# Cross-attention on one core: the context products of two groups in one set of 512-column matmuls, and scaling factors spread from rows written four times

## The chip, the cores and the metric

The kernel runs on one core of a Trainium2 chip. The core's engines work at the same time, each through its own instructions in order: TensorE (PE, matmuls), VectorE (DVE), ScalarE (ACT), GpSimd (POOL) and SyncE (SP), which here issues every DMA. They wait for each other through semaphores. The metric is the device time of one launch in microseconds (us). Three runs of the kernel before gave 676.45 us as their median, from 675.78 to 676.48.

## The reference, cut to what matters

Eight batches of 256 queries and 256 keys of width 1024; 32 query heads of width 32 share 8 key/value heads, so four query heads form a group with one key/value head. LoRA terms are added to each weight.

```python
q = _lora_linear(hidden_states, Wq, Aq, Bq)     # (8, 256, 1024): 32 heads of 32
k = _lora_linear(traces, Wk, Ak, Bk)            # (8, 256, 256):   8 heads of 32
v = _lora_linear(traces, Wv, Av, Bv)
scores = jnp.einsum('bhqd,bhtd->bhqt', q, k) / jnp.sqrt(HD)
attn = jax.nn.softmax(scores, axis=-1)
context = jnp.einsum('bhqt,bhtd->bhqd', attn, v)
out = _lora_linear(context, Wo, Ao, Bo)
return hidden_states + out
```

## The kernel before, in words

**Units and slots.** A group of four heads in one batch is a unit `u`; there are 8 per batch, 64 in all. A unit takes four slots `c = 0..3`, a batch has 32 slots `s`, and each engine has its own function `slot(b, s, ...)` that says what it does in a slot, in this order:

- PE: `scores_t` (L1519: the transposed scores of unit `u-1`, one matmul of 512 columns); the slot's share of the projections (`group_step`, L1482 and L1484: three matmuls of 256 columns and three of 512); if `c == 0` the context product of unit `u-2` (`context`, L1524 to L1537); then `scores` for four slots ahead (L1502: two matmuls of 256 columns).
- ACT: `exp_turned` (L941: the exponentials of the transposed scores, into `probs_t`); in some slots `proj_high` (L914, L919: the high part of a projected group); `exps` for three slots ahead (L930: exponentials with row sums).
- DVE: `row_max` for three slots ahead (L1142); at `c == 0` `split_max` and `turn_max` (L1151, L1153, L1163), which also turn the reciprocals of the unit before; at `c == 3` `reciprocal` (L1170) and `normalize` of unit `u-2` (L1177); then `proj_lows` (for k L1126 and L1129, for q L1134 and L1136: the low part of a projected group, after ACT's high part); in slots 15, 16, 18 and 19 `input_low` (L1183).
- POOL: `place_max` at `c == 1`, the splitting of the inputs, and one copy of v per batch.

**Projection groups.** A batch projects twelve groups (`BODY`: q4 to q7 of the batch, then k0, k1, q0 to q3, v0, v1 of the next), each 24 steps deep, nine steps in a slot. They alternate between two PSUM banks. So the first matmul of group `j` waits on `proj_out` until DVE has written the low part of group `j-2` (L1616). Group 4 (k0) has its low part written in DVE's slot 17; group 6 (q0) starts in PE's slot 19. Group 7 (q1) has its low part written in slot 25; group 9 (q3) starts in slot 27. In batch 0 the same holds.

**The context product.** Two key tiles times four heads: eight fp32 matmuls `128x32` by `128x256`, which the trace shows as sixteen instructions. Each head has its own 32 columns of the array (`tile_position=(0, HD * h)`) and lands in its own 32 rows of one half of a PSUM bank (`ctx_bank`). `probs_t` holds two units. `normalize` multiplies the 128x256 result by `scales` into `ctx_stage`, and `store_ctx` writes it to DRAM.

**The scaling factors.** The reciprocals of the row sums are turned into four rows of 256. `put_rows` writes them to DRAM (L535), and `spread` reads them back with each row repeated for 32 partitions (L543): four outermost rows, 128 pieces of 1 KB.

**Stages.** Up to about 54 us the weights are prepared. The units' steady work runs to about 460 us, batch 0 to 6. Then comes batch 7, in which the output weights are prepared as well (its own order, `last_body`). From about 535 us the output products of batches 1 to 7 run (L1543, L1677).

Of the kernel before, what the change touches and what calls it, by code (L numbers as in the profile page):

```python
# [27 lines left out]
P = 128  # L28
NB = 8
S = 256  # L30
D = 1024
KT = D // P
HD = 32
NG = 8
GH = 4
# [59 lines left out]
SUM_RING = 4  # L95


def xattn(nc, xt, ct, xn, wq, wkv, wo, akv, bkv, aq, bq, a4o, b4o, out):
    with ExitStack() as ctx:
# [44 lines left out]
        def rows_of(tile, rows):  # L144
# [27 lines left out]
                          for i in range(2))  # L172
# [8 lines left out]
        ctx_bank = banks[:, 4, 0:S]  # L181
# [4 lines left out]
        r_dram = nc.dram_tensor("r_rows", [2, GH, S], F32, kind="Internal").ap()  # L186
# [76 lines left out]
        block = ctx.enter_context(nc.Block())  # L263

# [130 lines left out]
        def _(sp):  # L395
# [118 lines left out]
            def body(b, first, last):  # L514
# [4 lines left out]

                def store_ctx(g):  # L520
                    if first and g < 0:
                        return
                    wait(ctx_done, unit0 + (g + 1))
                    row = ctx_dram[b, g] if g >= 0 else ctx_dram[b - 1, g + NG]
                    sp.dma_start(row, ctx_stage[:, g % 2]).then_inc(ctx_stored[g % 2], DMA)
# [6 lines left out]
                def put_rows(g):  # L532

                    wait(turned_out, unit0 + (g + 2))
                    sp.dma_start(r_dram[g % 2], turned_sb[KM:KM + GH, (g + 1) % 2]).then_inc(r_stored[g % 2], DMA)  # L535

                def spread(g):

                    if first and g < 0:
                        return  # L540
                    wait(r_stored[g % 2], b * (4 * DMA) + DMA * (g // 2 + 1))
                    need(sp, ctx_done, unit0 + (g - 1))
                    sp.dma_start(scales[:, g % 2], r_dram[g % 2].unsqueeze(1).broadcast_to([GH, HD, S])  # L543
                                 ).then_inc(r_spread[g % 2], DMA)
# [13 lines left out]
                store_ctx(-2)  # L558
# [5 lines left out]
                spread(0)  # L564
                store_ctx(-1)
                stack_q(4, fills + 3, st0 + 4)
                put_rows(1)
                load_x(1)
                send(pos["q", 5, 0])
                load_x(2)  # L570
                spread(1)
                send(pos["q", 6, 0])
                store_ctx(0)
                stack_q(5, fills + 3, st0 + 8)
                put_rows(2)
                load_x(3)
                spread(2)
                send(pos["q", 7, 0])
                store_ctx(1)
                stack_q(6, fills + 4, st0 + 12)  # L580
                load_context(b + 2, 0)
                put_rows(3)
                load_context(b + 2, 1)
                load_context(b + 2, 2)
                send(pos["k", 0, 1])
                spread(3)
                load_context(b + 2, 3)
                store_ctx(2)
                send(pos["k", 1, 1])
# [3 lines left out]
                spread(4)  # L593
                send(pos["q", 0, 1])
                store_ctx(3)
                stack_q(0, fills + 5, st0 + 20)
                put_rows(5)
                send(pos["q", 1, 1])
                spread(5)
                store_ctx(4)  # L600
                send(pos["q", 2, 1])
                stack_q(1, fills + 5, st0 + 24)
                put_rows(6)
                spread(6)
                send(pos["q", 3, 1])
                store_ctx(5)
                stack_q(2, fills + 6, st0 + 28)
                put_rows(7)
                if b == NB - 2:
# [284 lines left out]
        def _(act):  # L894
# [40 lines left out]
            def exp_turned(b, u, j):  # L935

                t, hp = divmod(j, 2)
                act.wait_ge(st_mm, b * SLOTS + (4 * u + j + 1))
                if j == 0:
                    need(act, ctx_mm, b * NG + (u - 1))  # L940
                nc.scalar.activation(  # L941
                    probs_t[:, u % 2, t, 2 * hp:2 * hp + 2, :].rearrange("p a b -> p (a b)"),
# [124 lines left out]
        def _(dve):  # L1067
# [105 lines left out]
            def normalize(b, u):  # L1173
# [3 lines left out]
                nc.vector.tensor_tensor(ctx_stage[:, u % 2, :], ctx_bank, scales[:, u % 2, :],  # L1177
                                        ALU.mult).then_inc(ctx_done, 1)

# [112 lines left out]
            def slot(b, s, first, last):  # L1292
# [20 lines left out]
                if c == 3 and not (first and u < 2):  # L1313
                    normalize(b, u - 2)
# [113 lines left out]
        def _(pe):  # L1428
# [95 lines left out]
            def context(b, u):  # L1524
# [5 lines left out]
                for t in range(2):  # L1530
                    for h in range(GH):
                        last = nc.tensor.matmul(  # L1532
                            ctx_bank[HD * h:HD * (h + 1), :],
# [207 lines left out]
```

## Time and profile before

| | |
|---|---|
| median of 3 runs | 676.45 us |
| the profiled execution: its own time | 678.06 us |
| the profiled execution: span of its instructions | 676.3 us |
| mean granted TensorE clock | 0.947 |
| PE busy | 662.5 us, 98% of the span |
| DVE busy | 512.7 us, 76% |
| ACT busy | 467.6 us, 69% |
| POOL busy | 375.9 us, 56% |

The span runs from the first to the last instruction of the profiled execution; its own time holds 1.8 us more, which lie around it. Busy time is the union of an engine's instructions. The ends of matmuls are modelled, so neighbouring matmuls overlap in the rows, and the pace of PE is read from one start to the next. A granted clock of 0.95 is the level of 2.4 GHz as this core was granted it, 0.5 the level of 1.2 GHz.

### The profile page before, as it was taken

The page shows a single profiled execution, that of the slowest core. Times are in us where ns is not written, and L with a number is a line of the kernel's source. Part 1 is how long each engine was busy: PE and PEld are TensorE (multiplying, and loading weights), DVE is VectorE, ACT ScalarE, POOL GpSimd, SP SyncE. Part 2 cuts the span into 40 slices and gives each one's busy share as a digit, 9 for nine tenths or more (in the row PEclk, how much of TensorE's full clock was granted, in tenths as well). Part 3 has the DMA queues.
Part 4 walks back from the last instruction along what each step waited for, and adds up shares of the span by engine and source line. Part 5 has one row for each costly group of instructions (what it writes and reads, how often), then busy time and mean ns, then how long its engine had stood idle before and what let it go on. Part 6 is the DMA issues. An engine that isn't in the chain of part 4 may idle for free.

```text
span 676.3 us, 13385 instructions
## 1 busy us (share of the span) xinstructions
PE 662.5 (98%) x4220; PEld 528.2 (78%) x4220; DVE 512.7 (76%) x1161; ACT 467.6 (69%) x1462; POOL 375.9 (56%) x325
## 2 busy tenths in 40 slices
PE   9999999999999999999999999999899999999998
PEld 6798777877877887887887788787676788888886
DVE  4768887787788778778777877878887898855542
ACT  5558888888888888888888888887678443222220
POOL 3548785843762584386358438535867005776632
PEclk9999999999999999999999999999899999999999
DMA  8956655675665567556656646667676335655331
GB/s 268 355 171 211 207 182 164 196 212 167 174 197 183 158 195 227 162 179 195 198 149 201 210 157 183 197 187 211 186 225 205 107 120 172 202 187 186 126 121 66
DMA packets 103829, 125.07 MB, mean 185 GB/s; under 512 B 9280, under 2 KB 85312, under 8 KB 103760
## 3 DMA queue, kind: packets, MB, share of 16 engines
q1 hardware_dynamic: 103760, 124.23, 59.6%
q8 instruction: 34, 0.56, 0.3%
q14 instruction: 35, 0.29, 0.1%
HBM read 86.18 MB, written 38.01 MB: 184 GB/s over the span
## 4 chain that ended last, share of the span: by engine, by line
PE 82%; DVE 8%; ACT 4%; DMA 3%; issue 2%; SPq 1%; DVEq 0%
PE banks L1484 20%; PE banks L1677 17%; PE banks L1482 10%; PE banks L1502 9%; PE banks L1532 8%; PE banks L1519 8%; PE banks L1543 6%; DVE neg_max L1142 2%; ACT banks L930 2%; PE banks L1463 2%; DVE turned_sb L1163 2%; DMA raw<-xt 1%; PE banks L1450 1%; DVE max_parts L1151 1%; DMA raw<-ct 1%
## 5 line engine op out<-in xcount | busy, mean ns | idle before, releaser
L930 ACT ACTIVATE banks<-banks,neg_max 128x256 f32<-128x256 f32 x512 | 229.9, 452 | 29.8 <-DVE neg_max L1142 24.6
L812 POOL TENSOR_TENSOR q_stack<-turned_sb,head_mask 8x512 fp32r<-8x512 f32 x128 | 136.0, 1062 | 172.8 <-DVE turned_sb L1163 167.1
L1142 DVE TENSOR_REDUCE neg_max<-banks 128x2 f32<-128x512 f32 x256 | 175.0, 686 | 41.9 <-PE banks L1502 38.9
L941 ACT ACTIVATE probs_t<-banks 128x512 f32<-128x512 f32 x256 | 155.0, 605 | 48.4 <-PE banks L1519 48.0
L1484 PE MATMUL banks<-x_both,w_hi 128*128 128x512 f32 x448 | 162.9, 396 | 0.1
L1482 PE MATMUL banks<-x_both,w_lo 128*128 128x256 f32 x448 | 118.6, 280 | 0.0
L1502 PE MATMUL banks<-k_stack,q_stack 96*128 96x256 f32 x512 | 109.8, 296 | 0.7 <-DMA q_stack<-q_parts 0.7
L1502 PEld LDWEIGHTS banks<-k_stack,q_stack 96*128 96x128 f32 x512 | 81.3, 190 | 35.4 <-issue 25.8
L930 ACT ACTIVATION_READ_ACCUMULATOR banks<-banks,neg_max 128x1 f32 x512 | 106.7, 208 | 0.0
L1519 PE MATMUL banks<-q_stack,k_stack 104*128 104x512 f32 x256 | 102.4, 400 | 0.0
L1482 PEld LDWEIGHTS banks<-x_both,w_lo 128*128 128x128 f32 x448 | 84.5, 189 | 9.2
L1484 PEld LDWEIGHTS banks<-x_both,w_hi 128*128 128x128 f32 x448 | 82.8, 189 | 11.3 <-DVE q_stage L1136 0.4
L1532 PE MATMUL banks<-probs_t,v_sb 128*32 128x256 f32 x1024 | 70.3, 394 | 0.1
L1163 DVE STREAM_TRANSPOSE turned_sb<-max_parts 32x64 f32<-32x64 f32 x260 | 62.1, 239 | 5.5 <-DVE max_parts L1153 0.7
L1519 PEld LDWEIGHTS banks<-q_stack,k_stack 104*128 104x128 f32 x256 | 48.5, 189 | 0.6
L1532 PEld LDWEIGHTS banks<-probs_t,v_sb 128*32 128x32 f32 x1024 | 27.0, 110 | 27.6 <-issue 14.1
L1134 DVE TENSOR_TENSOR q_stage<-banks,q_stage 128x256 fp32r<-128x256 f32 x56 | 23.8, 425 | 30.2 <-ACT q_stage L914 30.1
L782 POOL TENSOR_TENSOR c_both<-raw,c_both 128x512 fp32r<-128x512 f32 x32 | 41.2, 1287 | 2.5
L873 POOL TENSOR_TENSOR stage<-stage,probs_t 128x512 f32<-128x512 f32 x18 | 27.2, 1527 | 27.3 <-DVE probs_t L1380 17.9
L1484 PE MATMUL banks<-wkv_both,c_both 128*128 128x512 f32 x112 | 40.9, 397 | 0.3 <-DVE q_stage L1136 0.3
L1484 PE MATMUL banks<-c_both,wkv_both 128*128 128x512 f32 x112 | 40.6, 396 | 0.0
L772 POOL TENSOR_TENSOR c_both<-raw,ones 128x512 fp32r<-128x512 f32 x32 | 33.4, 1044 | 9.6 <-issue 7.5
(156 smaller groups left out, 1154.7 us busy)
## 6 DMA issues: line engine op xcount, KB each, us to landing
q_stack<-q_parts SPq DMA_DIRECT2D x192, 128.0 KB, 3.0
q_parts<-q_stage SPq DMA_DIRECT2D x64, 256.0 KB, 3.5
raw<-ct SPq DMA_DIRECT2D x32, 256.0 KB, 3.5
raw<-xt SPq DMA_DIRECT2D x32, 256.0 KB, 3.8
scales<-r_rows SPq DMA_DIRECT2D x64, 128.0 KB
context<-ctx_stage SPq DMA_DIRECT2D x64, 128.0 KB, 3.7
stage<-xn SPq DMA_DIRECT2D x16, 512.0 KB, 5.4
w_hi<-context SPq DMA_DIRECT2D x14, 512.0 KB, 7.0
```

The costliest lines, as they stand in the source:

```text
L782: nc.gpsimd.tensor_tensor(cols[1], raw[:, j, :], cols[0], ALU.subtract).then_inc(ready, 1)
L812: nc.gpsimd.tensor_tensor(q_stack[rows, u % RING, heads], turned_sb[rows, u % 2].unsqueeze(1).broadcast_to([M_ROWS, 2, S]), head_mask[rows ...
L930: last = nc.scalar.activation(score_bank(s)[:, S * h:S * (h + 1)], score_bank(s)[:, S * h:S * (h + 1)], ACT.Exp, bias=neg_max[:, u % 2, i: ...
L941: nc.scalar.activation(probs_t[:, u % 2, t, 2 * hp:2 * hp + 2, :].rearrange("p a b -> p (a b)"), st_bank[j % 2], ACT.Exp, scale=-1.0).then ...
L1142: nc.vector.tensor_reduce(out=neg_max[:, u % 2, 2 * c:2 * c + 2], in_=score_bank(s).rearrange("p (h t) -> p h t", h=2), axis=AXIS, op=ALU. ...
L1163: last = nc.vector.transpose(rows[:, :, HD * i:HD * (i + 1)], max_parts[HD * i:HD * (i + 1)])
L1482: mm = nc.tensor.matmul(proj_bank[bank][:, 0:S], still, moving[:, 0, kt, cols], start=False, stop=False)
L1484: mm = nc.tensor.matmul(proj_bank[bank].rearrange("p (a n) -> p a n", a=2), still, moving[:, :, kt, cols], start=(k == 0), stop=(k == GROU ...
L1502: last = nc.tensor.matmul(score_bank(s)[:, S * h:S * (h + 1)], q_stack[0:3 * HD, u % RING, 2 * hp + h, P * qh:P * (qh + 1)], k_stack[0:3 * ...
L1519: nc.tensor.matmul(st_bank[j % 2], k_stack[0:KM, u % NG, P * t:P * (t + 1)], q_stack[0:KM, u % RING, 2 * hp:2 * hp + 2, :].rearrange("p a ...
L1532: last = nc.tensor.matmul(ctx_bank[HD * h:HD * (h + 1), :], v_sb[:, t, HD * (u % NG):HD * (u % NG + 1)], probs_t[:, u % 2, t, h, :], start ...
L1677: mm = nc.tensor.matmul(product_bank(p), form_room[p][:, 512 * a_part + P * kt:512 * a_part + P * (kt + 1)], wo_forms[weight][w_part][:, k ...
```

## The change

For units 0 to 53 (`PAIRED`) the context products of two units run together. They are issued at `c == 0` of an odd `u`, for units `u-3` and `u-2`; at an even `u` nothing is issued. One matmul takes one key/value head and, as its moving operand, the probabilities of two query heads of that group (`j::2`): 512 columns. The four column strips of the array hold group `u` heads 0 and 2, group `u` heads 1 and 3, and the same of group `u+1`. So a pair of units needs 8 matmuls of 512 columns where it needed 16 of 256. A whole PSUM bank takes the result, and one `normalize_pair` of 128x512 stands for two `normalize` of 128x256, at `c == 3` of the odd `u`. A third buffer of probabilities, in `w_sum`, holds the unit that is being computed meanwhile.

The rows of `context` in DRAM have another order, and `wo` and `a4o` are laid out to match. The factors are written in four copies (16 rows of 1 KB), so that a spread reads eight outermost pieces, with 2 KB for each of 64 partitions. A spread for either unit of a pair waits until the pair before is normalized. SP's order in a batch is new: `store_pair` (two DMAs) replaces two `store_ctx`, and the spreads come later in the queue; `spread(1)` stands after the sending of q6, `spread(3)` after both sendings of k, and `spread(5)` after those of q1 and q2. Units 54 to 63 run singly as before; their `store_ctx` writes two blocks of 64 rows.

```diff
+COPIES = 4
+PAIRED = NB * NG - NG - 2
...
-        ctx_bank = banks[:, 4, 0:S]
+        ctx_bank = banks[:, 4, :]
...
-        r_dram = nc.dram_tensor("r_rows", [2, GH, S], F32, kind="Internal").ap()
+        r_dram = nc.dram_tensor("r_rows", [4, COPIES * GH, S], F32, kind="Internal").ap()
...
+        def p_buf(n):
+            if n >= PAIRED:
+                return p_room[(n + 1) % 2]
+            return p_room[(n + 1) % 3]
+        def contexts_before(n):
+            if n >= PAIRED:
+                return n - 1
+            return n - 1 if n % 2 else n - 2
...
+                def store_pair(g):
+                    wait(ctx_done, unit0 + (g + 2))
+                    v, n = place_of(g)
+                    for i in range(2):
+                        sp.dma_start(ctx_dram[v, n + i], ctx_stage[:, i]).then_inc(ctx_stored[i], DMA)
...
+                    if unit0 + g < PAIRED:
+                        sp.dma_start(r_dram[g % 4].rearrange("(j r h) n -> h j r n", j=2, h=2),
+                                     rows.unsqueeze(1).broadcast_to([GH, COPIES, S])).then_inc(r_stored[g % 2], DMA)
...
+                    if unit0 + g < PAIRED:
+                        need(sp, ctx_done, unit0 + (g - g % 2))
+                        rows = P // 2 * (g % 2)
+                        sp.dma_start(scales[rows:rows + P // 2].rearrange("p a n -> p (a n)"),
+                                     r_dram[g % 4].rearrange("(j h) n -> j (h n)", h=2).unsqueeze(1).broadcast_to([2 * COPIES, HD // COPIES, 2 * S])
+                                     ).then_inc(r_spread[g % 2], DMA)
+                        return
...
+            def normalize_pair(b, u):
+                for i in range(2):
+                    dve.wait_ge(r_spread[i], b * (4 * DMA) + DMA * (u // 2 + 2))
+                    dve.wait_ge(ctx_stored[i], b * (4 * DMA) + DMA * (u // 2 + 1))
+                dve.wait_ge(ctx_mm, b * NG + (u + 2))
+                nc.vector.tensor_tensor(ctx_stage[:].rearrange("p a n -> p (a n)"), ctx_bank,
+                                        scales[:].rearrange("p a n -> p (a n)"), ALU.mult).then_inc(ctx_done, 2)
...
-                if c == 3 and not (first and u < 2):
-                    normalize(b, u - 2)
+                if c == 3:
+                    if b * NG + u - 2 >= PAIRED:
+                        normalize(b, u - 2)
+                    elif u % 2 and b * NG + u - 3 >= 0:
+                        normalize_pair(b, u - 3)
...
+            def context_pair(b, u):
+                need(pe, ctx_done, b * NG + u)
+                pe.wait_ge(st_exp, b * SLOTS + (4 * u + 8))
+                if u == 0:
+                    pe.wait_ge(v_moved, b + 1)
+                for t in range(2):
+                    for k in range(4):
+                        g, j = u + k // 2, k % 2
+                        last = nc.tensor.matmul(
+                            ctx_bank[HD * k:HD * (k + 1), :].rearrange("p (h n) -> p h n", h=2),
+                            v_sb[:, t, HD * (g % NG):HD * (g % NG + 1)],
+                            p_buf(b * NG + g)[:, t, j::2, :], start=(t == 0), stop=(t == 1),
+                            tile_position=(0, HD * k))
+                last.then_inc(ctx_mm, 2)
...
-                if c == 0 and not (first and u < 2):
-                    context(b, u - 2)
+                if c == 0:
+                    if b * NG + u - 2 >= PAIRED:
+                        context(b, u - 2)
+                    elif u % 2 and b * NG + u - 3 >= 0:
+                        context_pair(b, u - 3)
```

## Rows read from the trace of the kernel before

**Rows 1.** The page, parts 1 and 4: busy time, the last chain.

```profile
PE 662.5 (98%) x4220; PEld 528.2 (78%) x4220; DVE 512.7 (76%) x1161; ACT 467.6 (69%) x1462; POOL 375.9 (56%) x325
...
PE 82%; DVE 8%; ACT 4%; DMA 3%; issue 2%; SPq 1%; DVEq 0%
```

**Rows 2.** Windows: length; PE, PEld, DVE, ACT, POOL busy; clock; DMA share, GB/s.

```profile
282.04:340.75 58.71, 58.71 (x418) 46.52 (x417) 46.86 (x125) 50.37 (x171) 32.31 (x29) 0.95 0.60 185
...
54.54:113.22 58.68, 58.25 (x402) 46.05 (x401) 48.83 (x122) 49.93 (x173) 44.27 (x40) 0.95 0.63 191
...
488.00:492.00 4.00, 4.00 (x21) 3.81 (x20) 2.56 (x7) 3.65 (x13) 3.77 (x4) 0.57 0.45 154
```

**Rows 3.** Timeline of PE, batch 4, slots 16 to 19: start, length.

```profile
312.57 0.28 PE L1482 MATMUL banks<-c_both,wkv_both 128*128 128x256 f32 x1
312.78 1.11 PE L1532 MATMUL banks<-probs_t,v_sb 128*32 128x256 f32 x16
313.81 0.50 PE L1502 MATMUL banks<-k_stack,q_stack 96*128 96x256 f32 x2
314.15 0.40 PE L1519 MATMUL banks<-q_stack,k_stack 104*128 104x512 f32 x1
...
315.44 0.40 PE L1502 MATMUL banks<-k_stack,q_stack 96*128 96x256 f32 x2
315.68 0.40 PE L1519 MATMUL banks<-q_stack,k_stack 104*128 104x512 f32 x1
...
317.45 0.40 PE L1484 MATMUL banks<-x_both,w_hi 128*128 128x512 f32 x1
```

**Rows 4.** Timeline of PE, two short windows within one context product.

```profile
305.69 0.86 PE L1532 MATMUL banks<-probs_t,v_sb 128*32 128x256 f32 x12
...
306.13 0.41 PE L1532 MATMUL banks<-probs_t,v_sb 128*32 128x256 f32 x4
```

**Rows 5.** Groups by form (busy us, mean ns | idle): plain fp32, 512 columns.

```profile
L1449 PE MATMUL banks<-probs_t,half_ident 128*128 128x512 f32 x26 | 13.9, 618 | 0.5 <-DVE w_lo L1095 0.5
```

**Rows 6.** Groups by form: the normalizing product of one unit.

```profile
L1177 DVE TENSOR_TENSOR ctx_stage<-banks,scales 128x256 f32<-128x256 f32 x64 | 23.9, 374 | 0.0
```

**Rows 7.** Timeline of DVE, batch 4, slots 15 to 17.

```profile
311.19 0.37 DVE L1177 TENSOR_TENSOR ctx_stage<-banks,scales 128x256 f32<-128x256 f32 x1
311.48 0.68 DVE L1183 TENSOR_TENSOR x_both<-raw,x_both 128x512 fp32r<-128x512 f32 x1
312.08 0.68 DVE L1142 TENSOR_REDUCE neg_max<-banks 128x2 f32<-128x512 f32 x1
...
315.56 0.41 DVE L1126 SCALAR_TENSOR_TENSOR k_stage<-banks,k_stage 128x256 fp32r<-128x256 f32 x1
316.01 0.42 DVE L1129 SCALAR_TENSOR_TENSOR k_stage<-banks,k_stage 128x256 fp32r<-128x256 f32 x1
```

**Rows 8.** Timelines of batch 0: DVE slot 17, PE slots 19 and 32.

```profile
80.84 0.42 DVE L1129 SCALAR_TENSOR_TENSOR k_stage<-banks,k_stage 128x256 fp32r<-128x256 f32 x1
...
81.40 0.41 PE L1484 MATMUL banks<-x_both,w_hi 128*128 128x512 f32 x1
...
106.28 0.50 PE L1484 MATMUL banks<-wkv_both,c_both 128*128 128x512 f32 x1 [0.27 <-DVE q_stage L1136]
```

**Rows 9.** Timeline of SP at a spread, and a window while it runs.

```profile
302.70 0.53 SPq L543 DMA_DIRECT2D scales<-r_rows  x1
305.03 0.36 SPq L439 DMA_DIRECT2D q_parts<-q_stage  x1
...
304.75:305.25 0.50, 0.50 (x5) 0.40 (x3) 0.50 (x2) 0.50 (x3) 0.33 (x1) 0.95 0.21 74
```

**Rows 10.** Timelines of batch 4, slots 24 to 27: DVE, then PE.

```profile
327.90 1.00 DVE L1163 STREAM_TRANSPOSE turned_sb<-max_parts 32x64 f32<-32x64 f32 x4
329.01 0.69 DVE L1142 TENSOR_REDUCE neg_max<-banks 128x2 f32<-128x512 f32 x1
...
332.11 0.39 PE L1484 MATMUL banks<-x_both,w_hi 128*128 128x512 f32 x1
```

More of the change, by code:

```diff
@@ L171, in xattn @@
         t1_raw, t2_raw = (probs_t[:, i].rearrange("p a b n -> p (a b n)").rearrange("p (a n) -> p a n", a=4)
-                          for i in range(2))
+                          for i in (1, 0))
+        p_room = [probs_t[:, 0], probs_t[:, 1],
+                  w_sum[:].rearrange("p a b -> p (a b)").rearrange("p (t h n) -> p t h n", t=2, h=GH)]
         t4_raw = t1_raw
@@ L518, in body, with place_of @@
                 fills = b * 4
+                def place_of(g):
+                    return (b, g) if g >= 0 else (b - 1, g + NG)
                 def store_ctx(g):
+                    wait(ctx_done, unit0 + (g + 1))
+                    v, n = place_of(g)
+                    rows = P // 2 * (n % 2)
+                    sp.dma_start(ctx_dram[v, n - n % 2:n - n % 2 + 2, rows:rows + P // 2],
+                                 ctx_stage[:, g % 2]).then_inc(ctx_stored[g % 2], DMA)
+                def store_pair(g):
                     if first and g < 0:
                         return
-                    wait(ctx_done, unit0 + (g + 1))
-                    row = ctx_dram[b, g] if g >= 0 else ctx_dram[b - 1, g + NG]
-                    sp.dma_start(row, ctx_stage[:, g % 2]).then_inc(ctx_stored[g % 2], DMA)
+                    wait(ctx_done, unit0 + (g + 2))
+                    v, n = place_of(g)
+                    for i in range(2):
+                        sp.dma_start(ctx_dram[v, n + i], ctx_stage[:, i]).then_inc(ctx_stored[i], DMA)
                 def load_x(*chunks):
@@ L534, in put_rows @@
                     wait(turned_out, unit0 + (g + 2))
-                    sp.dma_start(r_dram[g % 2], turned_sb[KM:KM + GH, (g + 1) % 2]).then_inc(r_stored[g % 2], DMA)
+                    rows = turned_sb[KM:KM + GH, (g + 1) % 2]
+                    if unit0 + g < PAIRED:
+                        sp.dma_start(r_dram[g % 4].rearrange("(j r h) n -> h j r n", j=2, h=2),
+                                     rows.unsqueeze(1).broadcast_to([GH, COPIES, S])).then_inc(r_stored[g % 2], DMA)
+                    else:
+                        sp.dma_start(r_dram[g % 4, 0:GH], rows).then_inc(r_stored[g % 2], DMA)
                 def spread(g):
@@ L557, in body @@
                 spread(-1)
-                store_ctx(-2)
                 stack_q(3, fills + 2, st0)
@@ L563, in body @@
                 send(pos["q", 4, 0])
-                spread(0)
-                store_ctx(-1)
                 stack_q(4, fills + 3, st0 + 4)
                 put_rows(1)
+                spread(0)
+                store_pair(-2)
                 load_x(1)
@@ L1715, in in_rows, with paired_rows @@
         return t
+    def paired_rows(a):
+        a = np.asarray(a)
+        return a.reshape(NG // 2, 2, 2, 2, HD, -1).transpose(0, 2, 1, 3, 4, 5).reshape(a.shape)
     x = np.asarray(inputs["x"])
@@ L1728 @@
         "bq": in_rows(80, w("Bq")),
-        "a4o": stacked(w("Ao").T),
+        "a4o": stacked(paired_rows(w("Ao")).T),
         "b4o": stacked(w("Bo")),
```

46 lines of the change are left out of this document (23 added, 23 removed).

## The prediction

> **What bounds the kernel now.** I read the page first: PE is busy 98% of the span and holds 82% of the chain that ended last [rows 1]. An average over stages can mislead, so I read windows next. In batch 4, a steady one, PE is busy 58.71 of 58.71 us, DVE 46.86 and ACT 50.37 [rows 2]. The change lies in batches 0 to 6, and there each tenth of a microsecond that PE is spared counts, as long as nobody else is late for it. Batch 0 differs: PE is busy 58.25 of 58.68 us, DVE 48.83 [rows 2], and at slot 32 PE stands waiting for DVE's low part of q [rows 8]. Then I read the timelines, PE's for the price of a context product and DVE's for how late it runs.
>
> **The price of a context product on PE.** In slot 16 the last projection matmul starts at 312.57 and the next `scores_t` at 314.15, which is 1.58 us [rows 3]. Between them lie one projection matmul and two of `scores`, all of 256 columns, and the product. Two of 256 columns take 0.24 (315.44 to 315.68 [rows 3]), so three take 0.36, and the product costs 1.22 us. Its sixteen instructions go in fours: from the second four (twelve left, 305.69) to the last (306.13) two steps of 0.22 pass [rows 4]. Four fours stream for 0.90. The rest, 0.32 us, lies at the edges: the product starts late (312.78, where 312.69 was due) and the two `scores` behind it take 0.34 instead of 0.24 [rows 3]; what is left stands between the last four and those `scores`.
>
> **What a pair costs.** The change halves the number of products and doubles their columns. For 512 columns of fp32, plain matmuls of the first stage show the pace: 26 in pairs cover 13.9 us, 1.07 a pair, and one lasts 0.62, so they start 0.45 apart [rows 5]. This is twice 0.225, so the stream is bound by columns, and a four of the new product should take 0.45. A pair is then 4 x 0.45 + 0.32 = 2.12 us, where two products took 2.44. The gain is 0.32 us a pair. Bounds: no less than the stream, 1.80, which would give 0.64; and no more than sixteen in a row without any overlap of strips, 7.2 us. I take 2.12, since fours of the same shape run four abreast in the rows.
>
> The Trainium skill, "TensorEngine Tiling (Array Packing)", Key Properties, says that a change of the tiling mode drains TensorE. By that rule the edges belong to going into the 32-column strips and out of them, once a product however many columns it has, and the sum is the one above; if they belonged to the columns instead, the gain would be nothing.
>
> **The sum without waits.** 54 units are paired, 27 pairs: 3 are issued in batch 0 (slots 12, 20, 28) and 4 in each of batches 1 to 6 (slots 4, 12, 20, 28). 27 x 0.32 = 8.6 us.
>
> **What the other engines do with it.** The products now stand in every second unit. PE runs seven slots without one, and the slots 0, 8, 16 and 24 come 1.22 us shorter. DVE and ACT used that time to catch up.
> - DVE saves nothing. One product of 128x256 takes 0.37 [rows 6] and the next instruction starts 0.29 after it (311.19 to 311.48); operations of 128x512 take 0.68 and start 0.60 apart (311.48 to 312.08 [rows 7]). Two of 0.29 become one of 0.60, and all of it stands at the end of the odd unit: DVE is 0.31 later in slots 7, 15, 23 and 31.
> - Slot 19 is where this collides. DVE runs without a gap from slot 15 on: normalizing at 311.19, input_low, row_max, and so on to the low part of k0, which ends at 316.01 + 0.42 = 316.43 [rows 7]. PE wants the bank that this frees at 317.45 [rows 3]. The slack is 1.02 us. The missing product of slot 16 takes 1.22 of it, and the later normalizing 0.31. PE waits 1.22 + 0.31 - 1.02 = 0.51 us, in each of batches 1 to 6: 3.1 us lost. Bounds: nothing (DVE finds 0.51 elsewhere), and 1.39 as below.
> - Slot 27 looks the same from afar. DVE turns until 328.90 and then waits for PE until 329.01 [rows 10]. In the new kernel it turns until 329.21 and goes on at once: row_max 0.60, the first low part 0.45 (315.56 to 316.01 [rows 7]), the second 0.42, done at 330.70 with the small steps between. PE comes at 332.11 - 1.22 = 330.89 [rows 10]. It just fits; I take no wait, with 0.3 a batch as the upper bound. Slots 3 and 11 have the same order of work and start with less backlog.
> - Slots 20, 4, 12 and 28 are 0.90 longer than before, so DVE and ACT catch up there.
> - Batch 0 has hardly any slack: the low part of k0 ends at 80.84 + 0.42 = 81.26 and PE takes the bank at 81.40 [rows 8], 0.14 us later. There 1.22 + 0.31 - 0.14 = 1.39 us of waiting stand against three pairs' 0.96. But DVE's work sets the pace of this batch, and PE already waits at slot 32 [rows 8]; what is lost at slot 19 is partly a wait that would have come later. I take batch 0 at nothing, between -0.4 and +1.0.
> - ACT has a third buffer and never waits for the pair. It needs 50.37 of 58.71 us [rows 2] and would need them of 57.4.
> - PE's own wait on `ctx_done` before a pair goes: the bank is normalized five slots earlier.
> - POOL's copy of v waits for the same product at the same slot 4.
>
> The Trainium skill, "VectorE: DVE Perf Modes", in its section on the TRN2 errata, gives an operation out of PSUM 120 cycles beside its columns at 0.96 GHz: 0.66 us for 512 columns, 0.39 for 256. By it the pair's normalizing would come 0.27 later and not the 0.31 of the rows, and the sum would be better by 6 x 0.04 = 0.2 us.
>
> **DMA and SP.** A spread issued at 302.70 is still moving at 304.75 to 305.25, with a DMA share of 0.21, 3.4 of 16 engines, as its four outermost rows suggest [rows 9]. With eight it should be done in about half that time. It was hidden and stays hidden. `spread(1)` is now issued behind the sending of q6, which went at 305.03 [rows 9]: at about 305.4. Even at the old pace (under 4 us) it lands by 309.4, and the pair is normalized at about 311.2 + 0.9 - 1.2 = 310.9. The cover is 1.5 us; if it went, DVE would wait and PE behind it, up to 0.5 us a batch. SP issues as many DMAs as before for each unit; the fourfold rows add 12 KB each, nothing beside a DMA share of 0.60 [rows 2].
>
> **Batch 7 and the end.** Units 54 to 63 run as before; all of it comes earlier. One part can jump: in the four us from 488.00 the granted clock is 0.57 [rows 2], that is, PE spends most of it at the 1.2 GHz level. At a level of 0.5 beside one of 0.95 that is (0.95 - 0.57) / 0.45 x 4 = 3.4 us of it, which cost about 1.7 us. It may come again, go, or come twice: 1.7 us either way, taken at nothing.
>
> **The sum.** 24 x 0.32 = 7.7, less 3.1, and batch 0 at nothing: 4.6 us. Against the profiled execution, 678.06 - 4.6 = 673.5 us (span 671.7); that execution stands 1.6 us above the median of the runs, so the time to expect is 676.45 - 4.6 = 671.8 us.
>
> **Rivals.**
> - A. PE keeps all of it: DVE's backlog gives way, and the 0.51 isn't seen. For it: DVE idles 11.9 us in batch 4 [rows 2]. Against it: none of that idle time lies between slots 15 and 17 [rows 7]. 676.45 - 8.6 = 667.9 us.
> - B. The waits take nearly all: slot 19 as forecast, slot 27 with 0.3 and slots 3 and 11 with 0.15 each, and one more stretch of the lower clock. 6 x (1.28 - 1.11) = 1.0 us gained, less 0.4 of batch 0 and up to 1.7: 676 to 677.5 us. No change to be measured.
> - C. Slower: DVE's backlog no longer empties in the long run of seven slots, and every batch goes as batch 0. It decides from 1.28 us of waiting a batch, the worth of four pairs. With 1.39 at slot 19 and 0.3 at each of the slots 3, 11 and 27 it is 2.3 a batch, 6 x 1.0 = 6 us lost: 682.5 us. For it: batch 0 is such a batch. Against it: steady batches give DVE 2 us more idle time than batch 0 [rows 2], and the longer products at slots 4, 12, 20 and 28 let it catch up.
> - D. The wide fours don't run four abreast (the change doesn't do what it says): 7.2 us a pair at worst, 27 x 4.8 = 130 us more. Nothing in the rows speaks for it.
>
> **Chances.** Forecast with its own range, 670.2 to 673.6: 0.50. Between that and no change, mostly by slot 27 and the clock: 0.11. A, 667 to 670.2: 0.22. B: 0.11. C and D: 0.06. A measurement of this kernel can tell about 0.2% (1.4 us) from no change. Faster by more than that 0.83, within it 0.11, slower 0.06. The range of 8 in 10 is 668.2 to 675.3.
>
> **What would show it.** In the profile after: products of x16 with 512 columns, about 2.05 us from the first start to the next `scores`, at slots 4, 12, 20 and 28 only; PE idle 0.4 to 0.6 us before L1484 in slot 19 of each batch, released by DVE's k_stage; a batch of 57.4 + 0.5 = 57.9 us instead of 58.7; no wait of DVE for a spread. The prediction is wrong if the fours start other than 0.45 apart, if the edges grow with the columns, or if PE waits in slots other than 19.

## The result, and the profile after

The kernel after takes 689.4 us (median of 687.95, 689.39 and 692.42; a fourth execution of 1639.4 us was disturbed and is left out, but the recorded median of 690.9, from which the expectations below count, includes it), the kernel before 676.1 beside it; the ratio is 1.020, with an interval of 1.0185 to 1.022. It is slower by about 2%, where 671.8 us were forecast. The profiled executions have spans of 687.6 and 676.3 us, 11.3 us apart, and the account below is of those.

The page after, parts 1 and 4:

```profile
PE 656.8 (96%) x3788; PEld 517.0 (75%) x3788; DVE 517.6 (75%) x1134; ACT 465.3 (68%) x1462; POOL 376.0 (55%) x325
...
PE 53%; DVE 18%; DMA 13%; ACT 7%; issue 4%; SPq 3%; POOL 0%; DVEq 0%; ACTq 0%; POOLq 0%
```

PE has 5.7 us less to do and still the span grew. PE's share of the chain fell from 82% to 53%; DVE and DMA took it [rows 1]. So the work was saved, and PE waits for others. The windows say where (batch 4; slot 4 of batch 0 to slot 4 of batch 1; the jump in batch 7; columns as in [rows 2]):

```profile
284.73:344.24 59.51, 57.59 (x355) 44.82 (x353) 47.53 (x121) 49.98 (x171) 31.97 (x29) 1.00 0.62 184
55.16:112.92 57.76, 56.23 (x339) 44.34 (x338) 47.98 (x118) 49.22 (x170) 43.38 (x38) 1.00 0.63 191
504.00:520.00 16.00, 12.84 (x59) 9.31 (x58) 8.39 (x21) 9.64 (x32) 6.23 (x6) 0.79 0.61 191
```

In batch 4 PE is busy 57.59 us instead of 58.71, and idle 1.92 us instead of none. The second window is 0.9 us shorter than its like before, because slot 0 of batch 1 has lost its product and a wait of 0.66 us; up to that slot batch 0 is longer. By the starts of `scores_t` in PE's timelines, the 11.3 us lie as follows (us; start of slot 0 to start of slot 0, batch 0 from its slot 4; the rest runs from the end of batch 7 to the end of the span):

| stretch | before | after | difference |
|---|---|---|---|
| up to slot 4 of batch 0 | 54.54 | 55.16 | +0.6 |
| batch 0 | 50.69 | 51.51 | +0.8 |
| batches 1 to 6 | 352.98 | 355.75 | +2.8 |
| batch 7 | 68.36 | 74.34 | +6.0 |
| the rest | 149.71 | 150.85 | +1.1 |

**The pair itself** is as forecast. PE's timeline at slot 12 of batch 4:

```profile
306.27 0.28 PE L1532 MATMUL banks<-x_both,w_lo 128*128 128x256 f32 x1
306.48 1.92 PE L1598 MATMUL banks<-probs_t,v_sb 128*32 128x512 f32 x16
308.33 0.51 PE L1552 MATMUL banks<-k_stack,q_stack 96*128 96x256 f32 x2
308.68 0.40 PE L1569 MATMUL banks<-q_stack,k_stack 104*128 104x512 f32 x1
```

Sixteen matmuls last 1.92 us, the last of them about 0.6: four start every 0.43 to 0.45. The `scores_t` before started at 305.10, so the slot takes 3.58 us, against 1.53 for one without a product: a pair costs 2.05 us, where two products cost 2 x 1.22 = 2.44. The gain is 0.39 us a pair, 9.4 in batches 1 to 6.

**Slot 19 and slot 24** take it back. PE's timeline of batch 4 shows both waits:

```profile
319.28 0.50 PE L1534 MATMUL banks<-x_both,w_hi 128*128 128x512 f32 x1 [1.04 <-DVE k_stage L1168]
...
331.15 0.50 PE L1552 MATMUL banks<-k_stack,q_stack 96*128 96x256 f32 x2 [0.88 <-DMA q_stack<-q_parts]
```

Slot 19 is longer than 1.53 us by 0.66, 1.39, 0.97, 1.30, 0.97 and 0.99 in batches 1 to 6, 6.3 us together; slot 24 by 1.55, 0.57, 1.28, 1.14, 1.64 and nothing, 6.2 us. Before, neither waited. 9.4 gained less 12.5 lost is the difference of the table, but for 0.3.

**Why slot 24: what SP issues, and when.** SP's timeline before, around the stacking of unit 7, and then the same of after:

```profile
320.40 0.33 SPq L405 DMA_DIRECT2D raw<-ct  x1
320.77 0.43 SPq L525 DMA_DIRECT2D context<-ctx_stage  x1
321.25 0.44 SPq L444 DMA_DIRECT2D k_parts<-k_stage  x1
321.79 2.61 SPq L429 DMA_DIRECT2D q_stack<-q_parts  x3
```

```profile
317.87 0.61 SPq L578 DMA_DIRECT2D scales<-r_rows  x1
318.84 0.81 SPq L553 DMA_DIRECT2D context<-ctx_stage  x2
319.71 1.04 SPq L421 DMA_DIRECT2D raw<-ct  x2
320.79 0.43 SPq L460 DMA_DIRECT2D k_parts<-k_stage  x1
321.27 2.25 SPq L421 DMA_DIRECT2D raw<-ct  x2
323.57 0.43 SPq L460 DMA_DIRECT2D k_parts<-k_stage  x1
324.10 0.63 SPq L578 DMA_DIRECT2D scales<-r_rows  x1
324.83 1.35 SPq L445 DMA_DIRECT2D q_stack<-q_parts  x3
```

Four loads of 256 KB stand in 3.8 us shortly ahead of the stack. Before, three of them had gone by 318 (their first at 313.62). The diff moved `load_context` 0 and 1 behind `spread(2)` and `store_pair(0)`, which the description of SP's new order leaves out. The stack is issued 11.6 us after the start of slot 16 (before: 10.4) and takes longer to land; the two answers for that line, before and after:

```profile
DMA to landing us min/median/max: 3.4/3.6/3.7
```

```profile
DMA to landing us min/median/max: 3.7/4.1/5.4
```

Counted from the start of slot 16, the last of its three DMAs landed at 15.2 us before and lands at 17.9 after. PE came to it at 17.1 before. Slots 16 and 24 have lost their products (2.3 us up to this point), slot 20 has a longer one (0.8) and slot 19 waits (1.3), so PE comes at 16.9. So it is the landing, 2.7 us later, that makes this wait. In batch 6, where the loads at this place fetch the context of batch 0 instead of inputs, the stack lands at 16.0 and slot 24 doesn't wait; why it lands sooner there is not shown.

**Why slot 19 waits twice as long as forecast.** DVE's timeline after, slot 15:

```profile
313.05 0.64 DVE L1224 TENSOR_TENSOR ctx_stage<-banks,scales 128x512 f32<-128x512 f32 x1
313.60 1.47 DVE L1230 TENSOR_TENSOR x_both<-raw,x_both 128x512 fp32r<-128x512 f32 x1
315.00 0.68 DVE L1181 TENSOR_REDUCE neg_max<-banks 128x2 f32<-128x512 f32 x1
```

and POOL's, after and then before:

```profile
311.25 3.28 POOL L808 TENSOR_TENSOR x_both<-raw,ones 128x512 fp32r<-128x512 f32 x3
```

```profile
309.42 3.64 POOL L772 TENSOR_TENSOR x_both<-raw,ones 128x512 fp32r<-128x512 f32 x3
```

Before, `input_low` took 0.68 [rows 7], and it was POOL's third operation that came out longer (3.64 for the three). After, POOL's three take 3.28 and `input_low` 1.47: it comes to an end 0.54 us after POOL's last (314.53). One of the two stands still in each of these rows, and the later normalizing (0.64 us) moved DVE behind the start of POOL's third. The Trainium skill, "SBUF — State Buffer", section "Who interferes with whom", says that a VectorE instruction with two SBUF inputs contends with a GpSimd instruction that reads SBUF, that the shared pair of ports is an exclusive lock, and that the order of issue decides who blocks. The trace agrees, but for the smallest distances: in batches 2 to 6 `input_low` starts 0.11 to 0.46 us behind POOL's third and pays 0.45 to 0.8 us, while in batches 0 and 1 it starts 0.01 and 0.02 us behind, still takes 0.68, and POOL's third takes 1.60.

**Batch 7.** Units 54 to 63 keep products of 256 columns, but their stores go to two half rows of a pair's place, so the store has two outermost rows. PE's timeline and SP's waits from 480 to 512 us after:

```profile
505.77 1.07 PE L1582 MATMUL banks<-probs_t,v_sb 128*32 128x256 f32 x16
509.83 0.79 PE L1552 MATMUL banks<-k_stack,q_stack 96*128 96x256 f32 x2 [2.98 <-DMA q_stack<-q_parts]
```

```profile
SPq L445 <- DMA q_parts<-q_stage: 8.4, 3, 4.0
SPq L583 <- DMA r_rows<-turned_sb: 8.1, 4, 3.6
```

The same two waits of SP took 2.9 and 1.2 us before. What is issued behind such a store lands late, SP waits for it, and PE stands for 2.98 us. The granted clock is at the 1.2 GHz level for 6.8 us from 508.6 on (hence 0.79 over those 16 us); before, batch 7 had one such piece of 3.4 us. Slots 20 and 21 take 7.53 and 3.00 us, before 3.16 and 1.87: 5.5 of the 6.0 us. (The writing of the rows has two outermost pieces since the change too, 16 KB each; in batches 1 to 6 SP waits nowhere for it.)

### The profile page after: what moved, and what is told of

It reads as the page before. It is cut to its first block, busy times and chain, and to the rows that moved or that the text cites. A ratio compares the mean times of both kernels' runs of the same rounds, so it can differ in the third digit from the quotient of the medians.

```text
span 687.6 us, 12494 instructions
## 1 busy us (share of the span) xinstructions
PE 656.8 (96%) x3788; PEld 517.0 (75%) x3788; DVE 517.6 (75%) x1134; ACT 465.3 (68%) x1462; POOL 376.0 (55%) x325
## 4 chain that ended last, share of the span: by engine, by line
PE 53%; DVE 18%; DMA 13%; ACT 7%; issue 4%; SPq 3%; POOL 0%; DVEq 0%; ACTq 0%; POOLq 0%
PE banks L1746 16%; PE banks L1534 12%; DMA q_stack<-q_parts 6%; PE banks L1532 6%; PE banks L1552 5%; PE banks L1598 5%; DVE neg_max L1181 4%; ACT banks L966 4%; PE banks L1569 4%; DMA q_parts<-q_stage 3%; DVE x_both L1230 3%; DVE turned_sb L1202 2%; DMA scales<-r_rows 2%; PE banks L1513 2%; PE banks L1499 2%
## 5 line engine op out<-in xcount | busy, mean ns | idle before, releaser
L980 ACT ACTIVATE probs_t<-banks 128x512 f32<-128x512 f32 x184 | 111.7, 607 | 37.9 <-PE banks L1569 36.2
L1552 PE MATMUL banks<-k_stack,q_stack 96*128 96x256 f32 x512 | 108.1, 293 | 9.8 <-DMA q_stack<-q_parts 9.7
L1598 PE MATMUL banks<-probs_t,v_sb 128*32 128x512 f32 x288 | 51.7, 598 | 0.0
L980 ACT ACTIVATE w_sum<-banks 128x512 f32<-128x512 f32 x72 | 43.8, 609 | 5.8 <-PE banks L1569 5.7
```

The lines of the kernel that those rows point to most:

```text
L980: nc.scalar.activation(p_buf(n)[:, t, 2 * hp:2 * hp + 2, :].rearrange("p a b -> p (a b)"), st_bank[j % 2], ACT.Exp, scale=-1.0).then_inc(s ...
L1552: last = nc.tensor.matmul(score_bank(s)[:, S * h:S * (h + 1)], q_stack[0:3 * HD, u % RING, 2 * hp + h, P * qh:P * (qh + 1)], k_stack[0:3 * ...
L1598: last = nc.tensor.matmul(ctx_bank[HD * k:HD * (k + 1), :].rearrange("p (h n) -> p h n", h=2), v_sb[:, t, HD * (g % NG):HD * (g % NG + 1)] ...
```

## The experiments

All are compared with the kernel before, run beside them.

**1. The last stores.** `e3_store` writes each of the ten stores as two DMAs of 64 partitions (the waits that count stores follow):

```diff
-sp.dma_start(ctx_dram[v, n - n % 2:n - n % 2 + 2, rows:rows + P // 2], ctx_stage[:, g % 2])
+for i in range(2):
+    sp.dma_start(ctx_dram[v, n - n % 2 + i, rows:rows + P // 2], ctx_stage[P // 2 * i:P // 2 * (i + 1), g % 2])
```

> The changed kernel with each of the ten stores of units 54 to 63 issued as two DMAs of 64 rows instead of one DMA with two outermost blocks. Theory: the one DMA runs on two DMA engines, keeps them busy for about 3 us, and what follows on them (rows of factors, q_parts) lands late; that is why batch 7 takes 6 us longer than before, with a wait of 3.0 us for q_stack in its slot 20 and the clock at the lower level for 6.8 us behind it. With two DMAs on all engines batch 7 is back within 1 us of before: 685 to 686 us against 690.9. Rival (batch 7 is late because it inherits late transfers and DVE's backlog from batch 6): no change, 690 to 691 us.

684.2 us, ratio 1.011 (1.008 to 1.013). That is 5.2 us back by the two medians (689.4) and 6.6 by the two ratios. Batch 7 takes 68.95 us (after: 74.34) and the rest 149.68, as before (149.71): 6.6 us by the profiled executions. The pieces at the 1.2 GHz level are gone from batch 7 with the wait. SP's wait for `r_rows` in the same window fell from 8.1 us to this:

```profile
SPq L584 <- DMA r_rows<-turned_sb: 0.9, 1, 0.9
```

The number of DMAs rose and the bytes stayed. The Trainium skill, "DMA: Bandwidth & Descriptors", section "Why a DMA increments its semaphore by 16 and not by 1", says that a DMA is split over as many engines, at most 16, as divide the outermost sizes of both sides: two for the store of the change, sixteen for these. The times agree; how many engines moved a store was not read.

**2. First repairs of slots 19 and 24, which made it slower.** `e1_sp` swaps neighbours in SP's order, `e2_low` moves all four low parts of the inputs; `e4_all` has both and the stores.

```diff
# e1_sp
-load_context(b + 2, 3); send(k1); spread(3); stack_q(7)
+send(k1); load_context(b + 2, 3); stack_q(7); spread(3)
# e2_low
-LOW_SLOTS = (15, 16, 18, 19)
+LOW_SLOTS = (17, 18, 19, 20)
```

> The changed kernel, with SP's order in a batch edited in one place: q6's and q7's transfers as they were, but the sending of k1 goes before the last load of the next context, and the loading of q_stack for unit 7 goes before spread(3). Theory: in the changed kernel PE waits about 1.1 us in slot 24 of batches 1 to 6 because that q_stack load is issued 2.7 us later against slot 20 than before; it stood behind a load that waits for DVE and behind the moved spread. With this order the load goes about 1.5 us earlier and the waits in slot 24 go, 5 to 6 us in all: 684 to 686 us against 690.9, with the waits of slot 19 and batch 7 left as they are. Rival (the transfers themselves are slower, because the new spreads and stores crowd the DMA engines): the load still lands 4 to 5 us after its issue and half or more of the wait stays, 688 to 690 us.

703.6 us, ratio 1.039 (1.0365 to 1.041): 14 us slower than after (12 by the ratios) instead of faster. The four loads still stood ahead of the stack: in batch 4 it was issued 1.1 us earlier and landed 0.3 earlier. So slot 24 kept most of its wait (4.7 of 6.2 us), and the spread behind it landed late. DVE's waits (us in total, times, longest):

```profile
DVE ctx_stage L1224 <- DMA scales<-r_rows: 17.5, 7, 3.1
```

That is once a batch, at slot 23, and PE stood behind it in slots 26 and 27.

> The changed kernel with DVE's four input_low of a batch moved from slots 15, 16, 18, 19 to slots 17, 18, 19, 20, where each stands behind that slot's low parts. Theory: in slot 19 PE waits for the low part of k0, 0.9 to 1.3 us in batches 2 to 6 and 0.6 in batch 1, because DVE has no gap between slots 15 and 17; with two input_low fewer ahead of it (2 x 0.6 us, and the 0.5 to 0.8 us by which the first of them was stretched beside POOL) the wait goes: 5 to 6 us less, 685 to 686 us. Against that, the input of q0 is ready later, which can bring up to 0.5 us a batch of new waiting in slot 19 or 20. Rival (DVE's backlog as such is the bound, wherever the work stands): the wait moves by a slot or two and nothing is gained, 689 to 691 us.

700.5 us, ratio 1.0365 (1.032 to 1.041). PE now waits for the low parts themselves:

```profile
PE banks L1534 <- DVE x_both L1230: 14.5, 21, 1.1
```

> The changed kernel with all three edits: k1's sending and q_stack's load of unit 7 earlier, input_low in slots 17 to 20, stores of units 54 to 63 as two DMAs. Theory (three separate causes): the three gains add up, 690.9 - 5.5 - 5.5 - 5 = about 675 us, and what is left of the 9 us that the pairs spare PE should bring it to 668 to 673 us if the waits go wholly. Rival (one bound, DVE's backlog, shows in all three places): 683 us or more.

707.3 us, ratio 1.043 (1.040 to 1.0465): the harm of both. What I had not seen is that spread, stack, loads and low parts all have a time at which someone wants them, and two of these times were nearer than the one that I mended.

**3. The loads put back.** On `e3_store`:

```diff
# g1_loads
 stack_q(6)
+load_context(b + 2, 0)
 put_rows(3)
+load_context(b + 2, 1)
 spread(2)
 store_pair(0)
-load_context(b + 2, 0)
-load_context(b + 2, 1)
# g2_early (without the above)
-load_context(b + 2, 3); send(k1); spread(3); stack_q(7)
+spread(3); stack_q(7); load_context(b + 2, 3); send(k1)
```

> e3_store (684.2 us) with the loads of context chunks 0 and 1 put back to where the kernel before had them, ahead of the rows of unit 3 and behind them, instead of behind spread(2) and store_pair(0). The profile of e3_store waits for q_stack of unit 7 in slot 24 for 2.13, 1.66, 2.25, 0.96, 0.91, 1.28 and 0 us in its seven plain batches, 9.2 us in all; its two first loads are issued 6.5 us after the start of slot 16 (kernel before: 2.2 and 3.7), and everything behind them in the queue lands 5 us after its issue. Theory 'the loads were moved into the stretch where q_stack of unit 7 is due': 512 KB less stand ahead of it, it lands by 15 us instead of 16.3 to 17.9 after slot 16, and most of the 9.2 us goes: 675 to 678 us. Rival 'q_stack of unit 7 is issued too late whatever is ahead of it (11.6 us after slot 16)': 682 to 685 us.

680.4 us, ratio 1.005 (1.003 to 1.007): 3.8 us less than `e3_store`, where 6 to 9 were expected. The profiled executions differ by 6.6 (span 676.5 against 683.1), but 1.0 of that lies ahead of batch 0, where the edit does not reach, and the one of `g1_loads` (678.42 us) is among the fastest of its ten (678.3 to 682.8). Batches 1 to 6 differ by 5.4. PE's waits for the stack, `e3_store` and then `g1_loads`:

```profile
PE banks L1553 <- DMA q_stack<-q_parts: 8.7, 8, 2.0
```

```profile
PE banks L1553 <- DMA q_stack<-q_parts: 2.1, 3, 1.1
```

The stack is issued no earlier (11.6 us after slot 16) and lands by 16.2 instead of 17.7, in batch 4. So bytes ahead in the queue were the cause of most of this wait, and the rival "issued too late" is out; by the median, about half of what was expected came back.

> e3_store with the loads where they are, and instead spread(3) and the three stack_q(7) DMAs issued ahead of the load of chunk 3 and of the send of k1, some 3 us earlier. In e1_sp the spread went behind stack_q(7), landed 6.5 us after its issue, and VectorE stood 2.4 us at normalize_pair for it in each batch; here the spread goes first. Theory 'order of issue is what makes q_stack of unit 7 late': the 9.2 us of slot 24 go, 675 to 677 us. Rival 'bytes in the queue, not its place': it lands 1 us earlier at most, 680 to 683 us. If k1, now behind, is late for its own stack, a new wait shows in slots 26 to 28.

681.0 us, ratio 1.006 (1.0035 to 1.008); PE's wait for the stack 2.8 us in 4 places. Place in the queue does about as well as bytes: 3.2 us here, 3.8 there.

**4. Slot 19.** `g3_low` moves the second low part alone, behind k0's (`LOW_SLOTS = (15, 17, 18, 19)`); `g4_three` has this, the loads and the early stack.

> e3_store with the second low part of the inputs (LOW_SLOTS 15, 16, 18, 19 made 15, 17, 18, 19): in slot 17 it stands behind k0's two low operations instead of ahead of them. Theory 'slot 19 waits for VectorE's queue, 0.69 us of which is this operation': the waits of slot 19 (0.91, 0.97, 1.33, 0.98, 1.34, 1.00, 0.99 us) shrink by 0.6 each, 4 us in all: 679.5 to 681 us. Rival, from e2_low where four moved low parts made the PE wait for x_both in slots 19 and 20: the third and fourth low parts stay where they were, so none of that is expected; if it comes back, 684 us or more.

686.8 us, ratio 1.014 (1.011 to 1.018): not faster. PE's wait for k0 halved, 2.7 us against 5.7, but it waited for x_both in its place: slot 19 is no shorter (2.87 in batch 4, as in `e3_store`) and slot 20 longer by 0.27 in every batch. In batch 4 the moved operation took 1.29 us. Here, moving work within DVE's backlog moved only the wait.

> g1_loads, g2_early and g3_low together on e3_store. If their effects stand in different slots: slot 24 free (9.2 us) and slot 19 shorter by 0.6 us a batch (4 us): 670 to 672.5 us, below the kernel before (676.4) and at the time first forecast for the change. If slot 24's wait only moves on to other slots: 678 us or more.

688.9 us, ratio 1.019 (1.014 to 1.024). The load of chunk 1 waits for that low part. With it one slot later, SP stood at this load until 6.7 us after slot 16 (4.6 in `g1_loads`), and slot 24's waits were back.

So work had to leave the backlog. `h1_norm` moves one `normalize_pair` a batch from slot 15 to slot 14, where DVE idles:

```diff
-if c == 3:
+if c == (2 if u == 3 else 3):   # pairs; single units stay at c == 3
```

> g1_loads (680.4 us, span 676.5) with one normalize_pair of each batch, that of slot 15, moved to slot 14, where VectorE stands idle for 0.77 and 0.45 us; the other three stay in their slots. In g1_loads input_low of slot 15 starts 0.08 us after GpSimd's third x_both<-raw has started and takes 1.50 us in place of 0.68, and TensorE waits 0.98 to 1.35 us in slot 19 of most batches (6.7 us in all). Theory 'slot 19 waits for VectorE's backlog, made by the 0.64 us operation and by the 0.8 us that input_low then stands behind GpSimd': input_low starts 0.6 us earlier, under GpSimd's second operation, ends about 1 us earlier, and the waits of slot 19 shrink to 0.3 us or less: 674 to 676 us. Rival 'GpSimd has the same hold on it wherever it starts, and it ends when it did': 0 to 1 us, 679 to 681 us.

684.1 us, ratio 1.013 (1.010 to 1.017), 3.7 more than `g1_loads`. Its spread had not landed; DVE's timeline in slot 14 of batch 4:

```profile
312.06 0.69 DVE L1225 TENSOR_TENSOR ctx_stage<-banks,scales 128x512 f32<-128x512 f32 x1 [0.83 <-DMA scales<-r_rows]
```

So this run decides nothing about the backlog. `i1_spread` issues `spread(1)` ahead of `load_x(2)` and the send of q6:

> h1_norm (684.1 us) with spread(1) issued ahead of the load of input chunk 2 and the send of q6, 2.1 us earlier. In h1_norm normalize_pair, moved to slot 14, waited 0.64 to 1.84 us for its spread in all seven batches, and slot 19 kept its wait. Theory 'slot 19 waits for VectorE's backlog': with the spread landed, normalize_pair runs in VectorE's idle time, input_low of slot 15 starts at once, and the waits of slot 19 fall from 1.0 to 1.5 us to 0.4 or less: 7 us below h1_norm and 3 to 5 below g1_loads (680.4), 674 to 677 us. Rival 'what slot 19 waits for does not depend on normalize_pair': slot 19 keeps 0.9 us or more, 679 to 681 us as g1_loads.

678.9 us (the ratio can't be told from 1: 0.9999 to 1.0036), 5.3 less than `h1_norm`. Slot 19 waits 0.53, 0.54, 0.98, 0.35, 0.99 and 0.24 in batches 1 to 6, 3.6 us instead of 7.7 in `h1_norm` and 6.3 in `g1_loads`: the theory holds in part. In batches 3 and 5, the two with 0.98 and 0.99, `input_low` still met POOL's third operation and took 1.50 and 1.36 us. What was won came back at slot 24 (4.4 us for the stack, against 2.1 in `g1_loads`), which PE now reaches sooner. Hence both together:

> h1_norm with spread(3) and stack_q(7) ahead of the load of chunk 3 and the send of k1 as in g2_early. g1_loads and g2_early each left 2 to 3 us of slot 24's waits. If what is left is place in the queue: another 2 us below h1_norm, 672 to 674 us. If both had the same bytes to clear: no difference to h1_norm (within 1 us); if k1 and its stack come late in turn: slower by 1 to 3 us.

681.8 us, ratio 1.0085 (1.007 to 1.010), 2.3 below `h1_norm`, as if by place in the queue.

> i1_spread with spread(3) and stack_q(7) ahead of the load of chunk 3 and the send of k1. h2_both stood 2.3 us below h1_norm with the waits of slot 24 nearly gone. The same here: 1 to 3 us below i1_spread, 672 to 675 us, below the kernel before. If the gain is used up: within 1 us of i1_spread.

676.3 us, no difference to before (0.998 to 1.001), 2.6 below `i1_spread`. Its profile shows slot 19 in both forms. DVE in batch 3 and its POOL, then in batch 4:

```profile
248.22 0.69 DVE L1225 TENSOR_TENSOR ctx_stage<-banks,scales 128x512 f32<-128x512 f32 x1
...
250.33 0.64 DVE L1231 TENSOR_TENSOR x_both<-raw,x_both 128x512 fp32r<-128x512 f32 x1
```

```profile
248.06 3.81 POOL L809 TENSOR_TENSOR x_both<-raw,ones 128x512 fp32r<-128x512 f32 x3
```

```profile
306.06 0.69 DVE L1225 TENSOR_TENSOR ctx_stage<-banks,scales 128x512 f32<-128x512 f32 x1 [0.49 <-DMA scales<-r_rows]
...
308.16 1.49 DVE L1231 TENSOR_TENSOR x_both<-raw,x_both 128x512 fp32r<-128x512 f32 x1
```

```profile
305.82 3.28 POOL L809 TENSOR_TENSOR x_both<-raw,ones 128x512 fp32r<-128x512 f32 x3
```

In batch 3 the spread is there, `input_low` starts 2.27 us after the start of POOL's three, takes 0.64, and POOL's take 3.81; slot 19 takes 1.76. In batch 4 DVE waits 0.49 for the spread, starts 2.34 us after them, takes 1.49, and slot 19 takes 2.95. That is 1.2 us more: DVE starts 0.45 later in its batch (1.96 us after the start of slot 15, against 1.51), and 0.07 us of distance to POOL's operations make `input_low` 0.85 longer.

**5. The copies of the rows.** `h3_once` and `h4_eight` are `h1_norm` with `COPIES` 1 and 8, `i3_eight` is `i2_both` with 8.

> h1_norm with COPIES = 1: the rows of scaling factors are written once, and a spread has two outermost rows instead of eight; the bytes that reach the scales are the same. Theory 'outermost rows set how many of the 16 engines work on a transfer' (the last stores of the change, two outermost rows, cost 6.7 us that e3_store took back): the 128 KB of a spread land 2 us or more later, VectorE waits for scales<-r_rows at normalize_pair, and TensorE behind it: 4 us or more above h1_norm, 679 to 690 us. Rival 'a spread has time enough': within 1 us of h1_norm.

754.2 us, ratio 1.114 (1.111 to 1.1165): 70 us more than `h1_norm`, where 690 was the most that I named. With two outermost rows DVE waits at most pairs:

```profile
DVE ctx_stage L1225 <- DMA scales<-r_rows: 70.4, 22, 6.4
```

> h1_norm with COPIES = 8: the rows are written eight times (32 KB a unit in place of 16 KB), a spread has sixteen outermost rows. By the same theory a spread lands sooner by under 1 us, which nothing waits for: within 1 us of h1_norm. If the write of the rows, twice as long, or the load on the engines counts: 1 to 3 us above it.

680.0 us, ratio 1.006 (1.004 to 1.009), 4.1 below `h1_norm`: more than "within 1 us". The spreads of which `h1_norm` waited for eight land sooner, and in batches 4 to 6 DVE waits 0.1 to 0.6 instead of 0.8 to 1.8 (in batch 1 it waits 2.3 instead of 1.0). In the profiled executions more of the gain stands in slot 24, where the stack is wanted (0.5 us in batches 1 to 6 instead of 2.5), than in slot 19 (6.5 instead of 7.7).

> i2_both with COPIES = 8. h4_eight stood 4.1 us below h1_norm, where VectorE waited for a spread; here nothing should wait for one, so within 1 us of i2_both. If it is again 2 us or more below, spreads are still late somewhere.

673.6 us, ratio 0.9954 (0.994 to 0.997). It beats both kernels, by 2.8 us against before, and stands 2.7 below `i2_both`: a spread was still late there. Batch 4 of it:

```profile
278.96:336.52 57.56, 57.44 (x355) 44.82 (x353) 47.11 (x121) 49.75 (x171) 32.29 (x29) 1.00 0.66 193
```

PE is idle for 0.12 us. Batches 1 to 6 take 345.6 us, 7.4 less than before, but batch 7 takes 71.45, 3.1 more. The windows of batch 7 in `i3_eight` and in `i2_both`:

```profile
451.55:523.00 71.45, 62.61 (x415) 48.34 (x413) 58.51 (x134) 51.91 (x168) 47.54 (x41) 0.95 0.63 193
```

```profile
454.20:523.22 69.02, 60.23 (x415) 46.11 (x413) 58.00 (x134) 51.81 (x168) 47.61 (x41) 1.00 0.67 199
```

This execution of `i3_eight` had two pieces of 3.4 us at the 1.2 GHz level in batch 7, `i2_both` none and the kernel before one. PE is busy 2.4 us longer in it, which is nearly the whole difference of the two. So a part of the 3.1 us goes with the clock of this one execution; what brings such a piece is not shown.

## Why the prediction was wrong

- **The price of a pair** (2.12 us, gain 0.32) was right to 0.07 us: 2.05 and 0.39. The stream was put at 0.45 a four and is 0.43 to 0.45; the edges did not grow with the columns (2.05 less 4 x 0.43 leaves 0.33). Rival D is out.
- **"SP issues as many DMAs as before for each unit", taken as no cost, failed.** The count was right. The order was not looked at: SP's part of the diff moves two loads of 256 KB to right ahead of `stack_q(7)`, and the step only asked whether the spreads were in time. This is slot 24, 6.2 us in batches 1 to 6. `g1_loads`, which puts the loads back, took 6.6 of the 8.7 us of this wait away in the profiled executions, and 3.8 us of time by the medians.
- **"Units 54 to 63 run as before" failed.** Their store has another shape, with two outermost rows. `e3_store` took 6.6 us back by the ratios with nothing else changed. The rows for the rule were at hand: the prediction itself read four outermost rows as 3.4 engines [rows 9], and did not apply it to the store.
- **Slot 19 was sized at 0.51 us a batch and is 1.05.** DVE's lateness was summed to 0.15 us (batch 1, where `input_low` took 0.68, waits 0.66); what the sum left out is that a later `input_low` meets POOL's third operation and takes 1.1 to 1.5 us in place of 0.68 in batches 2 to 6. The worst batch measured 1.39; that the bound of the term was 1.39 too is chance, since it was made of batch 0's slack. That the wait is DVE's backlog is shown by `i1_spread` and `i3_eight`; that the extra part is the meeting with POOL is read from the rows of several kernels, and no run took POOL's operation away.
- **Slot 27, slots 3 and 11, batch 0.** In batches 1 to 6 slot 27 has up to 0.1 us, slots 3 and 11 up to 0.2, in batch 1 alone: as forecast. Batch 0, taken at nothing with a bound of 1.0, lost 0.8.
- **"No wait of DVE for a spread"** was not quite so: 4.5 us in the whole kernel after, at L1224. `spread(1)` had the 1.5 us of cover that was worked out, and `h1_norm`, which used 1.5 us of it, found it gone.
- **Rival C** (slower) got the sign and not the mechanism: DVE's backlog does empty in the long products (no wait worth naming outside slots 19 and 24). The rivals were about DVE, the strips and the clock. None was about SP's queue or the end, which hold over 12 us.

The terms as they came out, in batches 1 to 6: 9.4 gained, 6.3 lost at slot 19, 6.2 at slot 24; then 0.8 in batch 0, 6.0 in batch 7, 1.1 behind it (gone with `e3_store`), and 0.6 ahead of batch 0. The last is no effect of the change as far as the runs tell: that stretch took between 53.5 and 55.4 us in runs whose edits do not reach it. With the three large ones mended (`i3_eight`) slot 19 still waits 2.1 us in batches 1 to 6; 9.4 less 2.1 is 7.3, and they gain 7.4, where 4.6 were forecast. The kernel gains 2.8 in all by the medians.

## What to carry to other kernels

When an edit shortens PE's work in some slots, list for each shared queue what is issued ahead of the next thing that PE wants there, by bytes and by outermost rows, and compare its time of landing with PE's new, earlier time; an equal number of DMAs says nothing. Read every access pattern of the diff for its outermost size, also in the part that "stays as it was". And where one wait is removed, look for the next due time close behind it: here the stores, the loads, the spread and the stack had to be mended together before the kernel was no slower than before (`i2_both`), and two repairs tried alone cost 10 us and more.

## What the runs showed of the hardware

- The granted clock of a steady batch is 0.95 before [rows 2] and 1.00 after, and the pace of the matmuls did not move: slots without a product take 1.52 to 1.54 us in both. The 0.95 is no mark of work without pauses: in the last round the kernel before was granted 0.995 to 1.00 in all its 25 executions, which took 675.8 to 678.7 us.
- DVE's `input_low` and POOL's copy of the same shape hold each other up: one runs in its own time (0.64 to 0.68 us, or 1.04), and the other ends 0.55 us after it where DVE is the one that waits, 0.9 us where POOL is. By the records of after and of all runs in which the two meet like this, `input_low` won wherever it started up to 0.06 us behind POOL's operation (`i3_eight`) and lost from 0.07 us on (`g2_early`).
- The number of outermost rows of the spreads, at equal bytes of a spread, is worth 70 us here between two and eight, and 2.7 to 4.1 us between eight and sixteen, though the rows written for it grow from 16 to 32 KB.
- Two outermost rows in ten stores of 128 KB cost 5.2 us by the medians and 6.6 by the ratios and the profiled executions, mostly by what was queued behind them.
